# Graph attention on one core: turned tokens between k's units, moments of two graphs per chunk

## The chip, the cores and the metric

The kernel runs on one core of one Trainium2 chip. The metric is the device time of one execution in microseconds; the time before is the median of three runs.

## The reference

128 graphs of 128 tokens with 384 channels. Tokens are normalised and passed through a ReLU, projected to q, k and v, and each graph's 12 heads of 32 channels attend over its 128 tokens, with an adjacency matrix as bias (times beta) and as mask. The result is added to the input.

```python
h = jnp.maximum(_layernorm(x, axis=-1), 0.0)
q = _split_heads(h @ Wq + bq)        # and k, v alike
scores = jnp.einsum('bhqd,bhkd->bhqk', q, k) / jnp.sqrt(HD)
scores = scores + beta * adj_e
scores = jnp.where(adj_e > 0, scores, -9000000000000000.0)
probs = jax.nn.softmax(scores, axis=-1)
out = jnp.einsum('bhqk,bhkd->bhqd', probs, v)
x = x + out.transpose(0, 2, 1, 3).reshape(B, N, D)
```

## The kernel before

**Steps and chunks.** The 128 graphs are taken four at a time in 32 steps (`STEPS`; s is the step, `par` its parity). A step has 12 slots (`SLOTS`), called chunks here and numbered u = 0 to 11. In one chunk the attention of one graph's four heads is worked on (`HPC` = 4; three chunks a graph), while the projections of the step's own four graphs (512 tokens) are worked off between the attention's instructions. The attention of a step's graphs lags: it begins at chunk 3 of the following step (`LAG` = 3). Steps 1 to 30 hold everything: attention of earlier graphs, projections, and preparation of the next step's tokens. Step 0 has no attention, step 31 prepares no tokens, step 32 has only attention.

**The attention's round.** For chunk n: TensorE forms four score tiles in the one PSUM bank `ps_s` (L456), once VectorE has read those of chunk n-1. VectorE adds the mask, negates, and takes each row's minimum (`biased`, `neg_max`, L638, four instructions with an accumulator read each). ScalarE takes the exponentials (`probs`, L523, four). One chunk later TensorE transposes them into `ps_t` (L464), ScalarE rounds them to fp16 (`pT` high, L548), VectorE forms the remainder (`pT` low, L644). One chunk later again TensorE multiplies with v (L479 to L481) into `ps_o`. When a graph's third chunk is through, VectorE takes the reciprocal of the sums (L654) and scales (L659, `on`), GpSimd adds x (L334), and SyncE's queue stores.

**The units of a step.** `UNITS` (L43) lists the other work of TensorE in a step, in order: q0 q1 q2, k0 k1 k2, v0 v1, turn 0, v2, turn 1, v3, turn 2. A q or k unit is nine matmuls of 512 columns, a v unit nine of 384 (high and low parts of both operands: `PARTS`), a turn unit transposes one third of the channels of the next step's normalised tokens `hn` (four transposes, L415). L55 to L71 cut this list into 24 pieces of about equal cost (512 or 384 a matmul, 1024 a turn), two for each chunk; `ENDED[u]` lists the units that end in chunk u. The pieces go out between the attention's instructions (TensorE's `step`, L484 to L497): scores, first piece, transposed probs, second piece, values.

**The banks.** Every unit writes one of three PSUM banks, in rotation over the list and over the step's border (`BANK`, L74). A unit's bank is free when the unit three positions ahead has been read (`bank_free`, L389): for q and k when VectorE has formed the low part (`qk_low`), for v when ScalarE has copied it (`v_copied`), for a turn when VectorE has formed the low part of `hT` (`h_low`).

**Who reads a unit.** ScalarE, in the chunk where the unit ended, behind the exponentials and pT high: high part of q, k (L543), of `hT` (L530), or the copy of v (L538). VectorE, one chunk later, right behind `biased`: `low_parts(s, par, u - 1, ahead)`, that is L619 for q and k, L609 for `hT`. v units ask nothing of VectorE.

**VectorE's order in a chunk** (L663 to L687): `biased`; low parts of the units that ended in the chunk ahead; in chunks 2, 5, 8 and 11 the reciprocal; in chunks 0 to 3 `moments` of one graph of the next step (L586); in chunks 2, 5, 8 and 11 the scaling; in chunk 4 `mask_unlinked` (L598), in chunk 7 `mask_linked` (L603); in chunks 0 to 3 `variance` (L592); pT low.

**GpSimd's order in a step** (L336 to L366): split of the last v (L326, L328), bias added to x of graphs 0 and 1 (L319), the add of graph 2 of two steps ago, bias of graph 2, then `rstd_of` and `normalise` of the next step's tokens (L302 to L313; they wait for all four variances), the add of graph 3, bias of graph 3, the add of graph 0, splits of v0 and v1, the add of graph 1, the split of v2. A turn on TensorE waits for all four normalised graphs (`normed`, L413).

**SyncE's queue** (L257 to L278): two stores, the 12 DMAs that spread q over partitions (they wait for the last low q part), a store, loads of x and adj, a store, the 12 DMAs that spread k.

Of the kernel before, what the change touches and what calls it, by code (L numbers as in the profile page):

```python
# [21 lines left out]
def graph_attention_kernel(nc, x, adj, wq, bq, wk, bk, wv, bv, beta, out):  # L22
# [4 lines left out]
    CH = D // P  # L27
    G = 4
    STEPS = GRAPHS // G
# [10 lines left out]
    assert N == P and TOK == 512 and HPC * N == 512  # L40


    UNITS = ([("q", c) for c in range(CH)] + [("k", c) for c in range(CH)]  # L43
             + [("v", 0), ("v", 1), ("turn", 0), ("v", 2), ("turn", 1), ("v", 3), ("turn", 2)])
    NB = len(UNITS)
    PROJ = [u for u in UNITS if u[0] != "turn"]
    QK = 2 * CH
    NP = len(PROJ)


# [33 lines left out]
    with ExitStack() as ctx:  # L84
# [98 lines left out]
        qk_high = sem("qk_high")  # L183
        qk_low = sem("qk_low")
# [15 lines left out]
        def wait(eng, s, value):  # L200

            if value > 0:
                eng.wait_ge(s, value)
# [83 lines left out]
        @block.gpsimd  # L287
        def _(pool):
            pool.memset(ident[:], 0.0).then_inc(ident_zeroed, 1)
            pool.memset(ones[:], 1.0).then_inc(consts_set, 1)  # L290
            pool.wait_ge(ident_zeroed, 1)
            pool.affine_select(out=ident[:], in_=ident[:], compare_op=ALU.not_equal, fill=1.0, base=0,
                               pattern=[[-1, P]], channel_multiplier=1).then_inc(consts_set, 1)
            pool.memset(half[:], -0.5).then_inc(consts_set, 1)
            pool.wait_ge(consts_set, 3)

            def rstd_of(s):

                wait(pool, var_done, G * (s + 1))
                wait(pool, normed, G * s)  # L300
                pool.nop(nofuse=True)
                pool.tensor_scalar(var_eps[:], mean_var[:, :, 1], EPS, None, ALU.add).then_inc(eps_added, 1)  # L302
                pool.tensor_scalar(neg_mean[:], mean_var[:, :, 0], -1.0, None, ALU.mult).then_inc(eps_added, 1)
                pool.wait_ge(eps_added, 2 * (s + 1))
                pool.tensor_tensor(rstd[:], var_eps[:], half[:], ALU.pow).then_inc(rstd_done, 1)

            def normalise(s, par):

                pool.wait_ge(rstd_done, s + 1)
                wait(pool, h_turned, CH * s)  # L310
                pool.nop(nofuse=True)
                for j in range(G):
                    pool.tensor_scalar(hn[:, j, :], xs[:, par, j, :], neg_mean[:, j:j + 1], rstd[:, j:j + 1],  # L313
                                       ALU.add, ALU.mult).then_inc(normed, 1)

            def add_bias(s, par, j):
                wait(pool, x_in[par], 8 * (s - par) + 16)
                wait(pool, added, G * (s - 2) + j + 1)
                pool.tensor_tensor(xb[:, par, j, :], xs[:, par, j, :], bv_row[:], ALU.add).then_inc(xb_done, 1)  # L319

            def split_v(s, par, j):
                wait(pool, pv_done, SLOTS * (s - 2) + CH * (j + 1))
                pool.wait_ge(v_copied, G * s + j + 1)
                pool.nop(nofuse=True)
                v32 = v_f[:, j % 2].rearrange("p (h d) -> p h d", d=HD)
                pool.tensor_copy(v1[:, par, j, :, 0:HD], v32).then_inc(v_high, 1)  # L326
                pool.wait_ge(v_high, G * s + j + 1)
                pool.tensor_tensor(v2[:, par, j], v32, v1[:, par, j, :, 0:HD], ALU.subtract).then_inc(v_split, 1)  # L328

            def add_x(s, par, j):  # L330

                pool.wait_ge(scaled, G * s + j + 1)
                pool.wait_ge(xb_done, G * s + j + 1)
                pool.tensor_tensor(on[:, j % 2, :], on[:, j % 2, :], xb[:, par, j, :], ALU.add).then_inc(added, 1)  # L334

            def step(s, par):  # L336
                proj, attend = 0 <= s <= STEPS - 1, 1 <= s <= STEPS
                older = 2 <= s <= STEPS
                if 1 <= s <= STEPS:
                    split_v(s - 1, 1 - par, G - 1)  # L340
                if proj:
                    add_bias(s, par, 0)
                    add_bias(s, par, 1)
                if older:
                    add_x(s - 2, par, 2)
                if proj:
                    add_bias(s, par, 2)
                if 0 <= s <= STEPS - 2:
                    rstd_of(s + 1)
                    normalise(s + 1, 1 - par)  # L350
                if older:
                    add_x(s - 2, par, 3)
                if proj:
                    add_bias(s, par, 3)
                if attend:
                    add_x(s - 1, 1 - par, 0)
                if proj:
                    split_v(s, par, 0)
                    split_v(s, par, 1)
                if attend:  # L360
                    add_x(s - 1, 1 - par, 1)
                if proj:
                    split_v(s, par, 2)
                if s == STEPS:
                    add_x(s - 1, 1 - par, 2)
                    add_x(s - 1, 1 - par, 3)  # L366

            rstd_of(0)
            normalise(0, 0)
            w_c = w_raw[:, :, W_COLS[1]]  # L370
            pool.wait_ge(w_squared, 2)
            pool.wait_ge(qk_scaling, 9)
            pool.tensor_tensor(w_c, w_c, gap[:, 1:2, :].bitcast(F32).broadcast_to([P, CH, D]),
                               ALU.mult).then_inc(wk_scaled, 1)
            pool.wait_ge(w_squared, 3)
            pool.wait_ge(v_scaling, 6)
            for c in range(CH):
                w_c = w_raw[:, c, W_COLS[2]].rearrange("p (h d) -> p h d", d=HD)
                pool.tensor_tensor(w_c, w_c, v_scale[:].rearrange("p (h o) -> p h o", o=1).broadcast_to([P, HEADS, HD]),
                                   ALU.mult).then_inc(wv_scaled, 1)  # L380
            for par in range(2):
                for j in range(G):
                    pool.tensor_copy(v1[:, par, j, :, HD], v_scale[:]).then_inc(consts_set, 1)
            pool.wait_ge(bv_in, 16)
            run_steps(step)

        @block.tensor
        def _(pe):
            def bank_free(s, par, o):  # L389

                if s == 0 and o < PB:
                    pe.wait_ge(h_low, o + 1)
                    return
                before, last, here = s, o - 1, par
                while True:
                    if last < 0:
                        before, last, here = before - 1, NB - 1, 1 - here
                    unit = UNITS[last]
                    runs = before < STEPS - 1 or unit[0] != "turn"
                    if runs and BANK[here][last] == BANK[par][o]:  # L400
                        break
                    last -= 1
                kind, n = unit
                if kind == "turn":
                    wait(pe, h_low, CH * (before + 1) + n + 1)
                elif kind == "v":
                    wait(pe, v_copied, G * before + n + 1)
                else:
                    wait(pe, qk_low, QK * before + last + 1)

            def turn(s, bank, c):

# [169 lines left out]
        def _(dve):  # L582
            def moments(s, par, j):
                wait(dve, x_in[par], 8 * (s - par) + 16)
                wait(dve, var_done, G * (s - 1) + j + 1)
                dve.bn_stats(stats[:, j, :], xs[:, par, j, :]).then_inc(stats_done, 1)  # L586
# [26 lines left out]
            def low_part(s, par, o):  # L613

                kind, n = UNITS[o]
                bank = ps_p[BANK[par][o]]
                dve.wait_ge(qk_high, QK * s + o + 1)
                dst, b = (qT, 0) if kind == "q" else (kT, 1)
                dve.scalar_tensor_tensor(out=dst[:, 1, n, :], in0=bank[:], scalar=bias_qk[:, b, n:n + 1],  # L619
                                         in1=dst[:, 0, n, :], op0=ALU.add, op1=ALU.subtract).then_inc(qk_low, 1)  # L620
# [42 lines left out]
            def step(s, par):  # L663
                proj, ahead = 0 <= s <= STEPS - 1, 0 <= s <= STEPS - 2
                for u in range(SLOTS + (LAG + 3 if s == STEPS else 0)):
# [7 lines left out]
                        low_parts(s - 1, 1 - par, SLOTS - 1, s <= STEPS - 1)  # L673
                    if ended:
                        invert_sums(valued[1], valued[3] // CH)
                    if ahead and u < G:
                        moments(s + 1, 1 - par, u)
                    if ended:
                        scale_out(valued[1], valued[3] // CH)
                    if proj and u == 4:  # L680
                        mask_unlinked(s, par)
                    if proj and u == 7:
                        mask_linked(s, par)
                    if ahead and u < G:
                        variance(s + 1, u)
                    if turning:
                        p_low(turning[0], (u - LAG - 1) % 2)  # L687

# [88 lines left out]
```

## Time and profile before

| | |
|---|---|
| median of three runs | 1162.26 us (1161.06 to 1162.73) |
| the profiled execution's own time | 1160.99 us |
| its span | 1159.1 us |
| TensorE matmul, weight load: busy | 1089.7 us (94%), 902.9 us (78%) |
| VectorE busy | 972.2 us (84%) |
| ScalarE busy | 891.0 us (77%) |
| GpSimd busy | 578.6 us (50%) |
| DMA, share of 16 engines | 43.7% (main queue) |
| mean granted TensorE clock | 0.974 |

The profile is of one execution. The span runs from its first to its last instruction; the execution's own time is 1.9 us longer, and 1.27 us below the median of the runs. Matmuls are pipelined and their ends are modelled, so PE's busy share says little about how much of PE is used; the timeline of single instructions says more. A row of the timeline gives start, duration, engine, line, operation, what is written and read, how many instructions are merged, and in brackets the idle time of the engine ahead of it with what ended it.

### The profile page before, as it was taken

What the parts mean: (1) busy time and instruction counts of PE and PEld (TensorE: products, weight loads), DVE (VectorE), ACT (ScalarE), POOL (GpSimd) and SP (SyncE); (2) the same over time, 40 slices, a digit from 0 to 9 for tenths busy, and PEclk for the clock granted to TensorE, in tenths of its full rate; (3) what the DMA queues carried; (4) which work ended last, traced back from release to release, by engine and by line L of the source; (5) the groups of instructions that cost most, each with busy time, mean ns of one, the idle gap of its engine ahead of it and who ended that gap; (6) DMA issues with size and microseconds to landing.
All of it is one profiled execution on the core that took longest, in us unless ns stands there. A gap on an engine that the chain in (4) does not pass through costs nothing. (4 is left out here: it accounts for less than half of the span.)

```text
span 1159.1 us, 33776 instructions
## 1 busy us (share of the span) xinstructions
PE 1089.7 (94%) x10959; PEld 902.9 (78%) x10959; DVE 972.2 (84%) x4343; ACT 891.0 (77%) x2343; POOL 578.6 (50%) x756
## 2 busy tenths in 40 slices
PE   4899999999999999999999999999999999999986
PEld 2778878888878888787888887888888788888764
DVE  6578888888888888898888888888889888888865
ACT  2377888788787888787888878788877888887865
POOL 3735464454555454546545455545454554545331
PEclk9999999999999999999999999999999999999965
DMA  4444434554434455444455443445544444543320
GB/s 145 116 123 123 110 105 123 140 147 126 120 98 123 130 140 136 120 111 113 119 137 147 130 116 100 122 128 139 145 115 109 114 119 134 147 126 98 98 70 28
DMA packets 91038, 138.79 MB, mean 120 GB/s; under 512 B 15600, under 2 KB 66288, under 8 KB 90864
## 3 DMA queue, kind: packets, MB, share of 16 engines
q1 hardware_dynamic: 90336, 135.85, 43.7%
q8 instruction: 88, 1.44, 0.6%
q14 instruction: 86, 0.70, 0.2%
q10 hardware_dynamic: 528, 0.79, 0.2%
HBM read 35.91 MB, written 25.17 MB: 53 GB/s over the span
## 5 line engine op out<-in xcount | busy, mean ns | idle before, releaser
L523 ACT ACTIVATE probs<-biased,neg_max 128x128 f32<-128x128 f32 x1536 | 491.9, 391 | 222.8 <-DVE neg_max L638 186.0
L435 PE MATMUL ps_p<-hT,w 128*128 128x512 f32 x1728 | 527.1, 423 | 5.2 <-DVE qT L619 2.5
L644 DVE TENSOR_TENSOR pT<-ps_t,pT 128x512 f16<-128x512 f32 x384 | 262.9, 685 | 141.3 <-ACT pT L548 141.0
L334 POOL TENSOR_TENSOR on<-on,xb 128x384 f32<-128x384 f32 x128 | 129.2, 1009 | 471.8 <-DVE on L659 392.9
L638 DVE CUSTOM_DVE_ANT_0 biased<-ps_s,mask 128x128 f32<-128x128 f32 x1536 | 352.0, 285 | 6.3 <-PE ps_s L456 4.3
L435 PEld LDWEIGHTS ps_p<-hT,w 128*128 128x128 f32 x1728 | 294.2, 192 | 53.4 <-DVE hT L609 7.3
L435 PE MATMUL ps_p<-w,hT 128*128 128x384 f32 x1152 | 270.2, 357 | 30.4 <-DVE hT L609 30.4
L464 PE MATMUL ps_t<-ident,probs 128*128 128x128 f32 x1536 | 237.8, 279 | 3.1 <-ACT probs L523 1.5
L464 PEld LDWEIGHTS ps_t<-ident,probs 128*128 128x128 f32 x1536 | 193.9, 143 | 43.8 <-ACT probs L523 7.1
L548 ACT ACTIVATE pT<-ps_t 128x512 f16<-128x512 f32 x384 | 220.5, 574 | 1.2 <-PE ps_t L464 1.2
L435 PEld LDWEIGHTS ps_p<-w,hT 128*128 128x128 f32 x1152 | 186.8, 189 | 37.6 <-DVE hT L609 37.5
L479 PEld LDWEIGHTS ps_o<-v,pT 128*128 128x128 f16 x1536 | 122.8, 96 | 84.7 <-issue 73.9
L479 PE MATMUL ps_o<-v,pT 128*128 128x33 f16 x1536 | 160.3, 181 | 3.2 <-DVE pT L644 2.3
L456 PE MATMUL ps_s<-k_st,q_st 96*128 96x128 f16 x1536 | 150.7, 221 | 7.4 <-DVE neg_max L638 4.9
L481 PE MATMUL ps_o<-v,pT 128*128 128x32 f16 x1536 | 155.6, 177 | 0.0
L480 PE MATMUL ps_o<-v,pT 128*128 128x33 f16 x1536 | 155.6, 178 | 0.0
L319 POOL TENSOR_TENSOR xb<-xs,bv_row 128x384 f32<-128x384 f32 x128 | 128.8, 1017 | 8.9 <-POOL on L334 0.4
L638 DVE DVE_READ_ACCUMULATOR2_ANT neg_max<- 128x1 f32 x1536 | 127.7, 83 | 0.1
L480 PEld LDWEIGHTS ps_o<-v,pT 128*128 128x128 f16 x1536 | 125.5, 97 | 0.3
L481 PEld LDWEIGHTS ps_o<-v,pT 128*128 128x128 f16 x1536 | 124.1, 96 | 0.0
L328 POOL TENSOR_TENSOR v<-v_f,v 128x384 f16<-128x384 f32 x128 | 114.0, 891 | 10.3
L456 PEld LDWEIGHTS ps_s<-k_st,q_st 96*128 96x128 f16 x1536 | 90.5, 97 | 10.6 <-DVE neg_max L638 6.2
(62 smaller groups left out, 1034.9 us busy)
## 6 DMA issues: line engine op xcount, KB each, us to landing
q_st<-qT SPq DMA_DIRECT2D x384, 96.0 KB, 2.2
k_st<-kT SPq DMA_DIRECT2D x384, 96.0 KB, 2.2
out<-on SPq DMA_DIRECT2D x128, 192.0 KB, 2.1
xs<-in_x SPq DMA_DIRECT2D x31, 768.0 KB, 4.8
adjs<-in_adj SPq DMA_DIRECT2D x32, 256.0 KB, 5.1
xs<-in_x ACTq DMA_DIRECT2D x1, 768.0 KB, 7.6
k_st<-in_L_gnn_Wq SPq DMA_DIRECT2D x1, 576.0 KB, 5.9
k_st<-in_L_gnn_Wk SPq DMA_DIRECT2D x1, 576.0 KB, 9.2
```

The lines of the kernel that those rows point to most:

```text
L319: pool.tensor_tensor(xb[:, par, j, :], xs[:, par, j, :], bv_row[:], ALU.add).then_inc(xb_done, 1)
L334: pool.tensor_tensor(on[:, j % 2, :], on[:, j % 2, :], xb[:, par, j, :], ALU.add).then_inc(added, 1)
L435: mm = pe.matmul(dst, stationary, moving, start=m == 0, stop=m == MMS - 1)
L456: mm = pe.matmul(ps_s[:, i * N:(i + 1) * N], q_st[0:STACK, gp, i, c, j * N:(j + 1) * N], k_st[0:STACK, gp, i, c, j * N:(j + 1) * N], start ...
L464: mm = pe.transpose(ps_t[odd][:, i * N:(i + 1) * N], probs[:, odd, i, :], ident[:])
L479: pe.matmul(o, high, first, start=True, stop=False)
L480: pe.matmul(o, low, first, start=False, stop=False)
L481: mm = pe.matmul(o[:, 0:HD], high, second, start=False, stop=True)
L523: act.activation(probs[:, odd, i, :], biased[:, odd, i, :], ACT.Exp, bias=neg_max[:, odd, i:i + 1], scale=-1.0).then_inc(exp_done, 1)
L548: act.activation(pT[:, odd, 0], ps_t[odd][:].rearrange("p (h q) -> p h q", q=N), ACT.Copy).then_inc(p_high_done, 1)
L638: dve.tensor_tensor_reduce(out=biased[:, odd, i, :], in0=ps_s[:, i * N:(i + 1) * N], in1=mask[:, gp, v // CH, :], scale=-1.0, scalar=3.0e3 ...
L644: dve.tensor_tensor(pT[:, odd, 1], ps_t[odd][:].rearrange("p (h q) -> p h q", q=N), pT[:, odd, 0], ALU.subtract).then_inc(p_low_done, 1)
```

## The change

Three edits, with what follows from the first. The list of units becomes q0 q1 q2, k0, turn 0, k1, turn 1, k2, turn 2, v0 v1 v2 v3. Since a turn now stands among the k units, the count of q and k units is looked up in a table (`QK_AT`) where the position was used before. VectorE takes moments and variances of two graphs in each of chunks 0 and 1, instead of one in each of chunks 0 to 3. GpSimd runs `rstd_of` and `normalise` ahead of the add of graph 2 and of the bias of graph 2. The 24 pieces are cut anew from the new list by the same rule.

```diff
--- before.py
+++ after.py
@@ -40,11 +40,12 @@
     assert N == P and TOK == 512 and HPC * N == 512
 
 
-    UNITS = ([("q", c) for c in range(CH)] + [("k", c) for c in range(CH)]
-             + [("v", 0), ("v", 1), ("turn", 0), ("v", 2), ("turn", 1), ("v", 3), ("turn", 2)])
+    UNITS = ([("q", c) for c in range(CH)] + [(kind, c) for c in range(CH) for kind in ("k", "turn")]
+             + [("v", j) for j in range(G)])
     NB = len(UNITS)
     PROJ = [u for u in UNITS if u[0] != "turn"]
     QK = 2 * CH
+    QK_AT = {o: [u for u in UNITS if u[0] in "qk"].index(unit) for o, unit in enumerate(UNITS) if unit[0] in "qk"}
     NP = len(PROJ)
 
 
@@ -341,13 +342,13 @@
                 if proj:
                     add_bias(s, par, 0)
                     add_bias(s, par, 1)
+                if 0 <= s <= STEPS - 2:
+                    rstd_of(s + 1)
+                    normalise(s + 1, 1 - par)
                 if older:
                     add_x(s - 2, par, 2)
                 if proj:
                     add_bias(s, par, 2)
-                if 0 <= s <= STEPS - 2:
-                    rstd_of(s + 1)
-                    normalise(s + 1, 1 - par)
                 if older:
                     add_x(s - 2, par, 3)
                 if proj:
@@ -406,7 +407,7 @@
                 elif kind == "v":
                     wait(pe, v_copied, G * before + n + 1)
                 else:
-                    wait(pe, qk_low, QK * before + last + 1)
+                    wait(pe, qk_low, QK * before + QK_AT[last] + 1)
 
             def turn(s, bank, c):
 
@@ -614,7 +615,7 @@
 
                 kind, n = UNITS[o]
                 bank = ps_p[BANK[par][o]]
-                dve.wait_ge(qk_high, QK * s + o + 1)
+                dve.wait_ge(qk_high, QK * s + QK_AT[o] + 1)
                 dst, b = (qT, 0) if kind == "q" else (kT, 1)
                 dve.scalar_tensor_tensor(out=dst[:, 1, n, :], in0=bank[:], scalar=bias_qk[:, b, n:n + 1],
                                          in1=dst[:, 0, n, :], op0=ALU.add, op1=ALU.subtract).then_inc(qk_low, 1)
@@ -673,16 +674,18 @@
                         low_parts(s - 1, 1 - par, SLOTS - 1, s <= STEPS - 1)
                     if ended:
                         invert_sums(valued[1], valued[3] // CH)
-                    if ahead and u < G:
-                        moments(s + 1, 1 - par, u)
+                    if ahead and u < 2:
+                        for j in range(2 * u, 2 * u + 2):
+                            moments(s + 1, 1 - par, j)
                     if ended:
                         scale_out(valued[1], valued[3] // CH)
                     if proj and u == 4:
                         mask_unlinked(s, par)
                     if proj and u == 7:
                         mask_linked(s, par)
-                    if ahead and u < G:
-                        variance(s + 1, u)
+                    if ahead and u < 2:
+                        for j in range(2 * u, 2 * u + 2):
+                            variance(s + 1, j)
                     if turning:
                         p_low(turning[0], (u - LAG - 1) % 2)
```

## Rows read from the trace of the kernel before

**Rows 1.** The page, part 1: busy time, share of the span, instructions of TensorE.

```profile
PE 1089.7 (94%) x10959; PEld 902.9 (78%) x10959; DVE 972.2 (84%) x4343; ACT 891.0 (77%) x2343; POOL 578.6 (50%) x756
```

**Rows 2.** Who waited for whom: total us, times, longest us.

```profile
DVE pT L644 <- ACT pT L548: 141.0, 174, 1.3
...
PE ps_p L435 <- DVE hT L609: 30.4, 30, 1.1
```

**Rows 3.** Timeline of VectorE, chunks 5, 6 and 7 of a middle step: start, us, ...

```profile
544.88 0.28 DVE L638 CUSTOM_DVE_ANT_0 biased<-ps_s,mask 128x128 f32<-128x128 f32 x1
...
547.72 0.28 DVE L638 CUSTOM_DVE_ANT_0 biased<-ps_s,mask 128x128 f32<-128x128 f32 x1
...
549.89 0.69 DVE L644 TENSOR_TENSOR pT<-ps_t,pT 128x512 f16<-128x512 f32 x1 [1.25 <-ACT pT L548]
550.50 0.28 DVE L638 CUSTOM_DVE_ANT_0 biased<-ps_s,mask 128x128 f32<-128x128 f32 x1
...
551.34 0.75 DVE L619 SCALAR_TENSOR_TENSOR kT<-ps_p,bias_qk,kT 128x512 f16<-128x512 f32 x1
552.00 0.74 DVE L603 SCALAR_TENSOR_TENSOR mask<-adjs,beta_col,mask 128x512 f32<-128x512 f32 x1
552.68 0.69 DVE L644 TENSOR_TENSOR pT<-ps_t,pT 128x512 f16<-128x512 f32 x1
553.28 0.28 DVE L638 CUSTOM_DVE_ANT_0 biased<-ps_s,mask 128x128 f32<-128x128 f32 x1
```

**Rows 4.** Timeline of ScalarE, chunk 6 of that step.

```profile
548.10 1.28 ACT L523 ACTIVATE probs<-biased,neg_max 128x128 f32<-128x128 f32 x4 [1.07 <-PE ps_t L464]
549.29 0.57 ACT L548 ACTIVATE pT<-ps_t 128x512 f16<-128x512 f32 x1
```

**Rows 5.** Timeline of TensorE, chunk 10 of that step.

```profile
557.22 0.38 PE L456 MATMUL ps_s<-k_st,q_st 96*128 96x128 f16 x4
...
560.48 0.61 PE L435 MATMUL ps_p<-w,hT 128*128 128x384 f32 x2 [1.09 <-DVE hT L609]
...
561.25 0.38 PE L456 MATMUL ps_s<-k_st,q_st 96*128 96x128 f16 x4
```

**Rows 6.** Timeline of VectorE, chunk 10 of that step and the first of 11.

```profile
558.90 0.28 DVE L638 CUSTOM_DVE_ANT_0 biased<-ps_s,mask 128x128 f32<-128x128 f32 x1
...
559.74 0.69 DVE L609 SCALAR_TENSOR_TENSOR hT<-ps_p,hT 128x512 fp32r<-128x512 f32 x1
...
561.81 0.29 DVE L638 CUSTOM_DVE_ANT_0 biased<-ps_s,mask 128x128 f32<-128x128 f32 x1
```

**Rows 7.** Timeline of VectorE, chunks 0 to 3 of the next step.

```profile
564.61 0.28 DVE L638 CUSTOM_DVE_ANT_0 biased<-ps_s,mask 128x128 f32<-128x128 f32 x1
...
566.05 0.55 DVE L586 BATCH_NORM_STATS2 stats<-xs 128x6 f32<-128x384 f32 x1
566.69 0.18 DVE L592 BATCH_NORM_AGGREGATE mean_var<-stats 128x2 f32<-128x6 f32 x1
...
567.45 0.29 DVE L638 CUSTOM_DVE_ANT_0 biased<-ps_s,mask 128x128 f32<-128x128 f32 x1
...
570.25 0.28 DVE L638 CUSTOM_DVE_ANT_0 biased<-ps_s,mask 128x128 f32<-128x128 f32 x1
...
573.42 0.28 DVE L638 CUSTOM_DVE_ANT_0 biased<-ps_s,mask 128x128 f32<-128x128 f32 x1
...
576.24 0.28 DVE L638 CUSTOM_DVE_ANT_0 biased<-ps_s,mask 128x128 f32<-128x128 f32 x1
```

**Rows 8.** Groups by line, of TensorE: count, busy us, mean ns, idle before.

```profile
L435 PE MATMUL ps_p<-hT,w 128*128 128x512 f32 x1728 | 527.1, 423 | 5.2 <-DVE qT L619 2.5 <-DVE w L725 1.4
...
L435 PE MATMUL ps_p<-w,hT 128*128 128x384 f32 x1152 | 270.2, 357 | 30.4 <-DVE hT L609 30.4
```

**Rows 9.** Timeline of GpSimd in the step of rows 3: normalising.

```profile
543.69 2.81 POOL L313 TENSOR_SCALAR hn<-xs,neg_mean,rstd 128x384 f32<-128x384 f32 x4 [0.21 <-POOL rstd L305]
```

**Rows 10.** Timeline of TensorE, the first scores of all, in step 1.

```profile
59.64 0.38 PE L456 MATMUL ps_s<-k_st,q_st 96*128 96x128 f16 x4 [2.53 <-DMA k_st<-kT]
```

## The prediction

> **What bounds the kernel now.** I read the page first. TensorE (PE) is busy for 94% of the span [rows 1], which invites the reading that PE sets the time and that its gaps are what can be won. The list of waits names the largest gap of PE inside the steps: 30 times, 1.0 us each, it waits for a VectorE instruction that writes hT (the low part of turned tokens), and VectorE in turn waits 174 times, 141 us, for ScalarE's pT before its own pT [rows 2]. So I went to the timeline of one middle step and measured each chunk on VectorE, from one first `biased` to the next. I number chunks by u within the step (12 per step).
>
> Chunk 6 has nothing on VectorE but the attention work. It takes 550.50 - 547.72 = 2.78 us, and VectorE idles 1.25 us of it [rows 3]. What fills it is a round trip: `biased` of this chunk starts; 0.38 us later ScalarE's exponentials start (548.10); after them the high part of the previous chunk's pT (549.29, 0.57 us long) [rows 4]; then VectorE's low pT (549.89), 0.61 us until the next `biased` (550.50) [rows 3]. Every engine queue is in program order, so chunk u+1 can't begin earlier. This loop, at 2.78 us, is the floor of every chunk; PE is ahead of it: the scores of chunk 10 start at 557.22 [rows 5], VectorE takes them up at 558.90 [rows 6], 1.68 us later.
>
> A chunk costs more than 2.78 for one of two reasons. Either VectorE's other work delays its low pT past 2.17 us after the chunk's start: chunk 2 takes 573.42 - 570.25 = 3.17 [rows 7], chunk 5 2.84 [rows 3]. Or PE delivers the next scores late: that is chunk 10, 2.91 us. There PE waits 1.09 us for hT, runs two matmuls of v3, the values and the scores (560.48 to 561.25 [rows 5]), and `biased` starts at 561.81 [rows 6]. So the 1.09 us gap of PE costs the loop only 2.91 - 2.78 = 0.13 us.
>
> **The change, part by part.** I worked out the 24 pieces of a step by the cost rule at lines 55 to 71. Before, turn 0 is in chunk 9, turns 1 and 2 in 10 and 11; after, they lie in chunks 5, 6 and 8, and v0 to v3 end in 9, 10, 11, 11. Each low part is done by VectorE one chunk after its unit ended. No instruction is added or removed, no DMA either; all move.
>
> 1. Moments of two graphs in chunks 0 and 1, none in 2 and 3. Chunk 2 then holds a low q part, the reciprocal and the scaling, just as chunk 5 holds k's: 2.84 in place of 3.17, **-0.33**. Chunk 3 (576.24 - 573.42 = 2.82 [rows 7]) falls to the floor, **-0.04**. Chunk 0 (2.84 [rows 7]) loses the low part of turn 2 (0.60 us of VectorE) and gains one pair of moments. One pair with its variance takes 0.64 us to the variance's start [rows 7]; two take some 0.47 more, since consecutive independent instructions of VectorE start about 0.09 before the recorded end of the one ahead. From 0.84 (end of `biased`) this gives 0.84 + 0.47 + 0.64 + 0.10 = 2.05, below 2.17: covered by the round trip in chunks 0 and 1. Chunk 0 falls to the floor, **-0.06**, chunk 1 from 2.80, **-0.02**. If the cover fails (four instructions end to end: 2 x 0.55 + 2 x 0.18 = 1.46 us instead of 1.21) it is +0.1 for each.
>
> 2. Chunk 10 no longer waits for a turned bank: to the floor, **-0.13**. Chunk 11 (2.80 [rows 6, 7]) loses turn 1's low part: **-0.02**.
>
> 3. The bank wait comes back in chunk 6. Three banks rotate by position, so each unit waits for the one three ahead. Before, v3 (position 11) needed turn 0 (8). After, k2 (position 7) needs turn 0 (4): turn 0 is again in the first half of a chunk, and k2 starts again in the second half of the next, behind turn 1. Turn 0's low part again follows `biased`. So chunk 6 takes on the pattern of chunk 10: 2.91, and k2's two 512-column matmuls instead of v3's 384-column ones: means 423 and 357 ns [rows 8], 2 x 0.066 = 0.13. Chunk 6: 3.04, **+0.26**. Bounds: nothing (k2's start isn't late) and +0.4.
>
> 4. Chunk 7 is the price that I consider decisive. It already has VectorE full: low k part at 551.34, `mask` at 552.00, low pT at 552.68, next `biased` at 553.28 [rows 3], with no idle time. After the change k1 and turn 1 both end in chunk 6, so both low parts stand in chunk 7, ahead of the mask and of low pT. The low part of turned tokens is 0.69 us long [rows 6], of which 0.60 counts (a 0.75 us k part is followed after 0.66 [rows 3]). Nothing covers it: 2.78 + 0.60 = 3.38, **+0.60**. Behind it stand low pT, the next `biased`, and through it ScalarE. Bounds +0.5 and +0.7.
>
> 5. GpSimd. Normalising ends at 543.69 + 2.81 = 546.50 now [rows 9], in chunk 5. It is released two chunks, 5.6 us, sooner, so it ends near 540.9; the first turn after the change, PE's chunk 5, begins no earlier than 544.88 - 1.68 + 0.2 = 543.4 [rows 3, 5, 6]. Slack 2.5 us: nothing. The add of graph 2 that it is moved past (and its store on SP's queue) comes some 3 us later; the buffer is wanted by the scaling of chunk 8 only, and the spread of q behind that store waits for chunk 4 anyway. The two last v parts now end in one chunk, so GpSimd splits them back to back over the step's border: under 6 us into the new step, when the variances come. If all this cover went, PE's turn 0 would wait; the rival below prices it.
>
> 6. Step 0 and 1. Four moments ahead of the first low q part delay PE's first k by about 1 us, and turn 0 then waits for normalising. But PE waits 2.53 us at the first scores for the k_st DMA [rows 10], which begins no later: nothing, bounds -1 and +1.5 us.
>
> **Sum** per full step: -0.33 - 0.04 - 0.06 - 0.02 - 0.13 - 0.02 + 0.26 + 0.60 = +0.26 us. The 30 steps that both attend and look ahead give 7.8 us. Against the profiled execution's own 1160.99 that is 1168.8; its time stands 1.27 below the median of the runs, so by the median 1162.26 the forecast is **1170.1 us**, 0.7% slower.
>
> **A rule that speaks for the change.** Here the busiest engine's gap costs 0.13 of its 1.09 us [rows 5, 6]. The Trainium skill (Perfetto Trace Analysis, Identifying the Most-Contended Engine, with Optimization Strategy) says to take the engine of the highest occupancy and remove what its gaps wait for; it also warns that matmul busy time is a poor measure. By that rule PE's 30 us would be the prize; the trace disagrees.
>
> **Rivals.**
> - *PE sets the pace* (5%): the hT wait [rows 2] vanishes and its 30.4 us with it: 1132. For: 94% busy. Against: the 1.68 us by which PE leads the loop, and the wait's return in chunk 6.
> - *The overloaded chunk is made up for* (10%): VectorE and ScalarE are both late after chunk 7, have idle time in chunks 9 to 11, and regain the 0.60. The sum is then -0.34 a step: 1152, **faster**. It decides where the chunks behind an overloaded one fall below 2.78. Against: behind chunk 2 with its 3.17, chunk 3 still takes 2.82 [rows 7].
> - *No return of the bank wait in chunk 6* (10%): turn 0's low part is in time, the sum is 0.00: 1162, no change. It needs PE to lead by less than 0.6 us there; against it is the lead of 1.68 before chunk 10.
> - *Turned tokens late* (10%): GpSimd isn't done by chunk 5, or chunks 0 and 1 overflow. One chunk's length of 0.2 to 0.4 more per step: 1176 to 1182.
>
> **The numbers.** Forecast 65%, slower by over 0.2%, as is the last rival: 0.75. Within 0.2% (about what a measurement of this kernel can tell from no change): 0.10. Faster: 0.15. The range takes the forecast with its bounds (chunk 6 at +0.4, a tenth in chunks 0 and 1: 0.26 + 0.14 + 0.2, 1180; I stop at 1177, as both at once are unlikely) and, below, the case of no change: 1162 to 1177.
>
> **What would show it.** Right: chunk 7 near 3.4 and chunk 2 near 2.84 on VectorE; PE still waits for hT about 30 times, 0.6 to 1.2 us each, now before k2; chunk 10 at the floor; normalising ends before chunk 5. Wrong: a hT wait gone from PE's list, a chunk 7 under 3.1, chunks behind it under 2.7, or GpSimd's hn named as PE's releaser.

## Result and profile after

The changed kernel takes 1169.68 us (median of 4 runs, 1169.38 to 1170.34), the kernel before 1161.8 us beside it: ratio on record 1.0072, 95% interval 1.0061 to 1.0084 (the two medians alone divide to 1.0068). It is slower by 0.7%, as forecast (1170.1, 0.7%). The spans of the two profiles differ by 1167.5 - 1159.1 = 8.4 us.

From the page, part 1 (busy time and share of the span):

```profile
PE 1089.2 (93%) x10959; PEld 899.8 (77%) x10959; DVE 980.3 (84%) x4343; ACT 893.3 (77%) x2343; POOL 572.5 (49%) x756
```

TensorE does the same work [rows 1]; no engine's busy time tells where 8 us came from. VectorE's is 8.1 us higher with the same instructions, but that is a coincidence: the rise is spread thinly over all its groups, while the time went into two chunks, as the table below shows. From the list of waits (total us, times, longest us), the rows that answer to [rows 2]:

```profile
DVE pT L645 <- ACT pT L549: 143.7, 204, 1.6
...
PE ps_p L436 <- DVE hT L610: 24.1, 30, 1.2
PE ps_p L436 <- ACT v_f L539: 16.5, 15, 1.2
```

The wait for turned tokens has not gone: 30 times again, 24.1 us for 30.4. In the trace it is 1.17 us in odd steps and 0.47 us in even ones. A third row is new in this size: 15 times, 1.1 us each, TensorE waits for ScalarE's copy of v.

VectorE's timeline, chunks 6, 7 and the first of 8 of a middle step (answering to [rows 3, 6]):

```profile
550.03 0.28 DVE L639 CUSTOM_DVE_ANT_0 biased<-ps_s,mask 128x128 f32<-128x128 f32 x1
...
550.87 0.69 DVE L610 SCALAR_TENSOR_TENSOR hT<-ps_p,hT 128x512 fp32r<-128x512 f32 x1
552.21 0.69 DVE L645 TENSOR_TENSOR pT<-ps_t,pT 128x512 f16<-128x512 f32 x1 [0.66 <-ACT pT L549]
553.06 0.29 DVE L639 CUSTOM_DVE_ANT_0 biased<-ps_s,mask 128x128 f32<-128x128 f32 x1 [0.16 <-PE ps_s L457]
...
553.91 0.75 DVE L620 SCALAR_TENSOR_TENSOR kT<-ps_p,bias_qk,kT 128x512 f16<-128x512 f32 x1
554.58 0.68 DVE L610 SCALAR_TENSOR_TENSOR hT<-ps_p,hT 128x512 fp32r<-128x512 f32 x1
555.17 0.74 DVE L604 SCALAR_TENSOR_TENSOR mask<-adjs,beta_col,mask 128x512 f32<-128x512 f32 x1
555.83 0.69 DVE L645 TENSOR_TENSOR pT<-ps_t,pT 128x512 f16<-128x512 f32 x1
556.43 0.28 DVE L639 CUSTOM_DVE_ANT_0 biased<-ps_s,mask 128x128 f32<-128x128 f32 x1
```

Chunk 6 lasts 553.06 - 550.03 = 3.03 us, and its end is a wait for scores. Chunk 7 lasts 556.43 - 553.06 = 3.37 us: two low parts, the mask and low pT follow each other without idle time. Both were 2.78 before. In the even steps, where TensorE waits only 0.47 us in chunk 6, that chunk takes 3.03 us too: already here the length of the wait is not its cost.

The same chunk 6 on TensorE (answering to [rows 5]):

```profile
549.84 0.60 PE L416 MATMUL ps_p<-ident,hn 128*128 128x128 f32 x4
551.61 0.73 PE L436 MATMUL ps_p<-hT,w 128*128 128x512 f32 x2 [1.17 <-DVE hT L610]
...
552.50 0.38 PE L457 MATMUL ps_s<-k_st,q_st 96*128 96x128 f16 x4
```

Turn 1 goes out, k2 waits 1.17 us for turn 0's low part (550.87 + 0.69 = 551.56), and the scores follow 0.89 us after k2's start.

VectorE's timeline at the start of the next step, chunks 0 to 3 (answering to [rows 7]):

```profile
567.64 0.28 DVE L639 CUSTOM_DVE_ANT_0 biased<-ps_s,mask 128x128 f32<-128x128 f32 x1
...
568.48 1.02 DVE L587 BATCH_NORM_STATS2 stats<-xs 128x6 f32<-128x384 f32 x2
569.41 0.36 DVE L593 BATCH_NORM_AGGREGATE mean_var<-stats 128x2 f32<-128x6 f32 x2
...
570.48 0.29 DVE L639 CUSTOM_DVE_ANT_0 biased<-ps_s,mask 128x128 f32<-128x128 f32 x1
...
573.28 0.28 DVE L639 CUSTOM_DVE_ANT_0 biased<-ps_s,mask 128x128 f32<-128x128 f32 x1
...
576.11 0.28 DVE L639 CUSTOM_DVE_ANT_0 biased<-ps_s,mask 128x128 f32<-128x128 f32 x1
...
578.91 0.28 DVE L639 CUSTOM_DVE_ANT_0 biased<-ps_s,mask 128x128 f32<-128x128 f32 x1
```

Chunks 0 to 3 last 2.84, 2.80, 2.83 and 2.80 us. Two pairs of moments end by 569.77, ahead of low pT: covered. Chunk 2 is down from 3.17.

Worked out from both timelines for all of steps 3 to 30 (mean time from one first `biased` to the next, in us):

| chunk | 0 | 1 | 2 | 3 | 4 | 5 | 6 | 7 | 8 | 9 | 10 | 11 |
|---|---|---|---|---|---|---|---|---|---|---|---|---|
| before | 2.84 | 2.80 | 3.18 | 2.83 | 2.80 | 2.83 | 2.79 | 2.79 | 2.84 | 2.79 | 2.92 | 2.80 |
| after | 2.82 | 2.80 | 2.83 | 2.81 | 2.80 | 2.83 | 3.05 | 3.38 | 2.84 | 2.79 | 2.80 | 2.79 |

A step goes from 34.19 to 34.54 us in the mean, 0.35 more. Steps 2 to 30 together take 1001.7 us for 991.6, 10.1 more. The first scores of all come 1.8 us sooner (57.87 for 59.64 [rows 10]); step 1 gains another 0.4 and the two last steps lose 0.4. Together that is the 8.4 us of the spans.

Not all of the 0.35 is the change's. In step 32, which has only attention, a chunk lasts 2.789 us in this trace and 2.781 to 2.783 in the other eleven, among them the five of this same kernel with a small edit. Seven thousandths in each of 12 chunks are 0.08 us a step; why this execution has them stays open. That leaves about 0.27 for the change.

The same step 32 shows what the floor of a chunk is not. TensorE is granted half its clock there (0.50 from 1125 to 1150 us) and has no projections, and every chunk still takes the 2.78 or 2.79 us of a quiet chunk of the full steps. So neither TensorE nor the amount of other work sets the floor; that it is the round trip of `biased`, exponentials, high pT and low pT is read from the timelines, and no run shortens that trip.

### The profile page after: what moved, and what is told of

It is laid out like the page before. It is cut to its first block and busy times, and to the rows that moved or that the text cites. A ratio compares the mean times of both kernels' runs of the same rounds, so it can differ in the third digit from the quotient of the medians.

```text
span 1167.5 us, 33776 instructions
## 1 busy us (share of the span) xinstructions
PE 1089.2 (93%) x10959; PEld 899.8 (77%) x10959; DVE 980.3 (84%) x4343; ACT 893.3 (77%) x2343; POOL 572.5 (49%) x756
## 5 line engine op out<-in xcount | busy, mean ns | idle before, releaser
L436 PE MATMUL ps_p<-hT,w 128*128 128x512 f32 x1728 | 530.0, 423 | 45.8 <-DVE hT L610 24.1
L436 PEld LDWEIGHTS ps_p<-hT,w 128*128 128x128 f32 x1728 | 291.1, 191 | 91.3 <-DVE hT L610 31.2
L436 PE MATMUL ps_p<-w,hT 128*128 128x384 f32 x1152 | 261.9, 354 | 0.0
L327 POOL CAST v<-v_f 128x384 f16<-128x384 f32 x128 | 64.9, 507 | 112.3 <-issue 102.5
```

The lines of the kernel that those rows point to most:

```text
L436: mm = pe.matmul(dst, stationary, moving, start=m == 0, stop=m == MMS - 1)
```

## The experiments

Each was timed against the kernel before on its own chip; I give that ratio and the interval. Means of chunks are taken over steps 3 to 30, as above. The theory under test: every chunk is a round trip VectorE, ScalarE, VectorE of at least 2.79 us, and what a chunk takes beyond it, by VectorE's work or by late scores, is never regained.

**a1_mask6**: the changed kernel, chunk 7 relieved.

```diff
-                    if proj and u == 7:
+                    if proj and u == 6:
                         mask_linked(s, par)
```

> The changed kernel with one edit: the second half of the mask (mask_linked) is taken in chunk 6 instead of chunk 7. The loop theory (every chunk lasts at least 2.79 us, a VectorE overload in one chunk adds to the time in full and is never regained): chunk 7 holds biased 0.84, two low parts 0.66 and 0.60, low pT 0.60, so it falls from 3.37 to 2.79; in chunk 6 the mask (0.68) fits behind turn 0's low part while PE's scores are awaited, so chunk 6 stays 3.03. 30 x 0.58 = 17 us off: 1152, faster than both kernels. Rival, the cost lies in TensorE's waits and not in VectorE's chunk 7: within 2 us of 1169.7. Rival, a late chunk is made up for behind it: the same, within 2 us of 1169.7.

Measured: 1151.35 us, ratio 0.993 (0.9916 to 0.9945): faster than the kernel before, against 1.0072 with the mask in chunk 7. Chunk 7 on VectorE, from its first `biased` to the next:

```profile
545.20 0.29 DVE L639 CUSTOM_DVE_ANT_0 biased<-ps_s,mask 128x128 f32<-128x128 f32 x1 [0.16 <-PE ps_s L457]
...
547.99 0.28 DVE L639 CUSTOM_DVE_ANT_0 biased<-ps_s,mask 128x128 f32<-128x128 f32 x1
```

2.79 us, as computed; chunk 6 stays 3.03. The two ratios differ by 1.4%, some 16.5 us, for the 17 expected. Both rivals fall: the instruction moved by one chunk, no work went, and the late chunk had not been made up for.

**a2_one_each**: the changed kernel, moments one graph a chunk again, and the variances alike.

```diff
-                    if ahead and u < 2:
-                        for j in range(2 * u, 2 * u + 2):
-                            moments(s + 1, 1 - par, j)
+                    if ahead and u < G:
+                        moments(s + 1, 1 - par, u)
...
```

> The changed kernel with the moments put back to one graph in each of chunks 0 to 3 (units and GpSimd's order as changed). The loop theory: chunk 2 goes from 2.83 back to 3.17, chunk 3 by 0.03, and now the tokens are late: the last variance ends some 2.2 us into chunk 3, normalising takes GpSimd some 5 us more, so turn 0 in PE's chunk 5 waits over 2 us and chunk 5 grows by about 1.7; some 2 us a step, 1225 to 1235. Rival, GpSimd is in time anyway and only chunk 2 pays: 0.37 x 30 = 11 us, 1181. Rival, where the moments stand makes no difference: 1170.

Measured: 1275.55 us, ratio 1.1001 (1.0979 to 1.1023). The direction is right, the size is not: 40 us above the top of the range. On TensorE, turn 0 of one step and turn 1 of the same:

```profile
601.86 1.08 PE L416 MATMUL ps_p<-ident,hn 128*128 128x128 f32 x4 [3.15 <-POOL hn L314]
605.59 0.38 PE L457 MATMUL ps_s<-k_st,q_st 96*128 96x128 f16 x4
607.23 0.60 PE L416 MATMUL ps_p<-ident,hn 128*128 128x128 f32 x4
```

The stretch from 600 to 604 us (busy times, then the granted clock):

```profile
600.00:604.00 4.00, 2.14 (x8) 1.87 (x9) 2.40 (x12) 1.33 (x5) 3.86 (x6) 0.66 0.10 37
```

After waiting 3.15 us TensorE was granted 0.66 of its clock there, so a part of the stretch ran at the 1.2 GHz level: four transposes take 1.08 us instead of 0.60, and the next scores start 3.73 us after the turn does, for 2.56 in the changed kernel. Chunk 5 lasted 6.2 us in odd and 5.6 us in even steps on average, not the 4.5 that I had worked out at full clock. The steps themselves separate the wait from the clock. In steps 6, 12, 14, 16, 18 and 24 TensorE waited 2.6 to 2.9 us and its clock stayed at 1.00 throughout chunk 5: the chunk took 4.7 us. In the other 23 of steps 2 to 30 it waited 2.6 to 3.2 us, the clock fell, and the chunk took 5.8 to 6.9 us. All six are even steps, and beside the even steps with the same wait the lower clock costs 1.3 to 2.2 us. So with the clock at full my sum was near, 4.7 for 4.5, and the lower clock is most of the missing 40 us; in odd steps, where the wait was 3.0 to 3.2 us, the clock fell every time, so the two aren't told apart there. The Trainium skill (TensorE: Matmul & The Clock Gate, What's actually happening) says that the clock follows how busy the array has lately been; this row agrees: TensorE had been idle for 3.15 us. The 1.17 us wait of the changed kernel doesn't do this: its clock in that stretch is 1.00.

So the units' new order needs tokens so early that the moments must come first: with GpSimd's order but without the moments edit it costs 10%. Whether it needs GpSimd's order too, no run tries. An estimate from the rows of the changed kernel says yes: with the add and the bias of graph 2 ahead of it, normalising could begin no sooner than 575.60 (end of VectorE's scaling) + 1.01 + 1.02 = 577.63, where it began at 572.81; it would end near 582.1 instead of 577.3, and turn 0 starts at 581.04, so it would be some 1.1 us late.

**b1_moments_only**: the kernel before with the moments edit of the diff alone.

> The kernel before with the moments edit alone (two graphs in each of chunks 0 and 1; old units, old order of GpSimd). The loop theory: chunk 2 from 3.17 to 2.84 and chunk 3 by 0.03 shorter, but chunk 0 still holds the low part of turn 2: 0.84 + 0.60 + 0.47 + 0.64 + 0.10 + 0.60 = 3.25, 0.41 over 2.84. Sum +0.04 a step, no change: 1161 to 1164. Rival, the moments edit is a gain by itself and the order of units the whole cost: 0.37 x 30 = 11 us off, 1151.

Measured: 1158.27 us, ratio 0.9992 (0.9983 to 1.0002), no change. Chunk 0 on VectorE:

```profile
562.31 0.28 DVE L638 CUSTOM_DVE_ANT_0 biased<-ps_s,mask 128x128 f32<-128x128 f32 x1
...
563.15 0.69 DVE L609 SCALAR_TENSOR_TENSOR hT<-ps_p,hT 128x512 fp32r<-128x512 f32 x1
563.75 1.01 DVE L586 BATCH_NORM_STATS2 stats<-xs 128x6 f32<-128x384 f32 x2
564.68 0.36 DVE L592 BATCH_NORM_AGGREGATE mean_var<-stats 128x2 f32<-128x6 f32 x2
564.95 0.66 DVE L644 TENSOR_TENSOR pT<-ps_t,pT 128x512 f16<-128x512 f32 x1
565.53 0.28 DVE L638 CUSTOM_DVE_ANT_0 biased<-ps_s,mask 128x128 f32<-128x128 f32 x1
```

3.22 us for the 3.25 computed. What chunk 2 gains (0.35) chunk 0 pays (0.37), both in the mean. It is the old turn 2, whose low part falls into chunk 0, that makes the same edit worthless here and a gain in the changed kernel.

**b2_chunk2_free**: the kernel before, moments and variances put where the round trip covers them.

```diff
-                    if ahead and u < G:
-                        moments(s + 1, 1 - par, u)
+                    for j in (((0,), (1, 2), (), (3,))[u] if ahead and u < 4 else ()):
+                        moments(s + 1, 1 - par, j)
...
```

> The kernel before with moments of graph 0 in chunk 0, graphs 1 and 2 in chunk 1, graph 3 in chunk 3, none in chunk 2. The loop theory: chunk 1 has room for two (low pT may start at 2.17, they end by 2.05), so chunk 1 stays 2.80, chunk 2 falls from 3.17 to 2.84, the rest stays: 0.33 x 30 = 10 us off, 1152. Rival, VectorE's chunk lengths are not what sets the step (its work is only moved, and it is idle elsewhere): 1162.

Measured: 1149.05 us, ratio 0.9911 (0.9896 to 0.9925), 10.1 us less than the kernel before on that chip, as computed. Chunks 1 and 2:

```profile
560.74 0.29 DVE L638 CUSTOM_DVE_ANT_0 biased<-ps_s,mask 128x128 f32<-128x128 f32 x1
...
563.53 0.28 DVE L638 CUSTOM_DVE_ANT_0 biased<-ps_s,mask 128x128 f32<-128x128 f32 x1
...
566.37 0.28 DVE L638 CUSTOM_DVE_ANT_0 biased<-ps_s,mask 128x128 f32<-128x128 f32 x1
```

2.79 and 2.84 us. Two instructions a step, the moments and the variance of graph 2, moved by one chunk; no unit touched.

**b3_mask6**: the kernel before with the mask's edit of a1_mask6.

> The kernel before with mask_linked in chunk 6 instead of chunk 7. The loop theory: chunk 7 was full but exactly at the floor (2.78), and chunk 6 has 1.25 us idle, so 0.68 us less in one and more in the other changes nothing: ratio 0.999 to 1.001. Rival, every busy microsecond of VectorE in a full chunk counts: 0.6 x 30 = 18 us off, ratio 0.985.

Measured: 1159.67 us, ratio 1.0001 (0.9992 to 1.001). The same edit gives 16 us to the changed kernel and nothing to this one, since chunk 7 was full but not over the floor.

**a3_cut**: the changed kernel, one matmul of k2 fewer in chunk 6.

```diff
-            ATOMS.append((o, 0, 2 * TOK))
+            ATOMS.append((o, 0, 3 * TOK))
```

> The changed kernel with one number changed: a turn counts 3 x 512 instead of 2 x 512 when the units are cut into pieces. By this only one matmul of k2 instead of two goes out in chunk 6, and no unit ends in another chunk. The loop theory: in chunk 6 the chain biased, low part of turn 0, k2's matmuls, values, scores, biased loses one matmul of 512 columns, 0.24 us: 3.03 to 2.80. 30 x 0.24 = 7 us off the changed kernel: 1163, a ratio of 1.001 to the kernel before. Rival, PE's wait itself (1.1 us in odd, 0.5 in even steps) is the cost of chunk 6: it is as long as before, so no change: ratio 1.007.

Measured: 1162.88 us, ratio 1.0031 (1.0019 to 1.0042), between the two expectations and nearer to the loop's. Chunk 6 on TensorE and on VectorE:

```profile
548.58 0.50 PE L436 MATMUL ps_p<-hT,w 128*128 128x512 f32 x1 [1.29 <-DVE hT L610]
549.24 0.38 PE L457 MATMUL ps_s<-k_st,q_st 96*128 96x128 f16 x4
```

```profile
547.00 0.28 DVE L639 CUSTOM_DVE_ANT_0 biased<-ps_s,mask 128x128 f32<-128x128 f32 x1
...
549.79 0.29 DVE L639 CUSTOM_DVE_ANT_0 biased<-ps_s,mask 128x128 f32<-128x128 f32 x1
```

TensorE waits longer, 1.29 us in odd steps for 1.17, and yet the chunk falls to 2.79 here and to 2.82 in the mean. The length of the wait isn't the cost; what stands between its end and the next scores is. Most of the missing 0.002: chunk 1 of every even step rose from 2.81 to 2.90, since the new cut gives it eight 512-column matmuls where TensorE has just lost its lead.

**a4_cut_mask6**: both edits.

> The changed kernel with the same cut (a turn counts 3 x 512) and mask_linked in chunk 6. The loop theory: both gains add, since they are in different chunks: 0.58 + 0.24 = 0.82 us a step off the changed kernel, 25 us: 1145, ratio 0.986. In chunk 6 the mask follows turn 0's low part and is not in the chain. Rival, with so much less in the loop PE becomes the bound (its lead was shrinking): ratio 0.990 or more.

Measured: 1149.16 us, ratio 0.991 (0.9893 to 0.9926): only 0.002 better than a1_mask6, intervals overlapping. The loop theory's 0.986 is missed and the rival's 0.990 or more came. TensorE in chunk 7:

```profile
542.46 0.38 PE L457 MATMUL ps_s<-k_st,q_st 96*128 96x128 f16 x4
542.65 1.18 PE L436 MATMUL ps_p<-hT,w 128*128 128x512 f32 x4
543.67 0.60 PE L465 MATMUL ps_t<-ident,probs 128*128 128x128 f32 x4
544.02 1.18 PE L436 MATMUL ps_p<-hT,w 128*128 128x512 f32 x4
545.36 0.38 PE L457 MATMUL ps_s<-k_st,q_st 96*128 96x128 f16 x4
```

Eight matmuls make it 2.90 us long. With a lead this is hidden (chunk 2 of the changed kernel has eight too, and lasts 2.83), but right behind a wait there is none, and chunk 7 lasts 2.90 on VectorE as well. Of the 0.21 us that chunk 6 gained over a1_mask6, chunks 7 (0.09) and 1 (0.05 in the mean) gave most back: the cut moved a matmul to where TensorE was the bound. So the loop theory holds only where TensorE has a lead; without one, a chunk of eight 512-column matmuls has a floor of its own, 2.90.

**a5_cut4_mask6**: mask in chunk 6 and a turn counted `4 * TOK`.

> The changed kernel with mask_linked in chunk 6 and a turn counted 4 x 512. Turn 0 then ends in chunk 4 beside k0, so its low part is in time for k2 and PE's wait in chunk 6 is gone; but chunk 5 holds two low parts, reciprocal and scaling: 0.84 + 0.66 + 0.60 + 0.25 + 0.48 + 0.60 = 3.43 in place of 2.83. The loop theory: +0.60 and -0.24 a step against the kernel with mask_linked in chunk 6 alone (ratio 0.993): 11 us more, ratio 1.002, though PE waits less. Rival, PE's waits for turned tokens are the cost: ratio 0.987 (7 us less).

Measured: 1164.82 us, ratio 1.0045 (1.003 to 1.006). From a1_mask6's 0.993 that is 13 us more, 11 expected. Chunk 5 on VectorE:

```profile
545.55 0.28 DVE L639 CUSTOM_DVE_ANT_0 biased<-ps_s,mask 128x128 f32<-128x128 f32 x1
...
548.98 0.28 DVE L639 CUSTOM_DVE_ANT_0 biased<-ps_s,mask 128x128 f32<-128x128 f32 x1
```

3.43 us as computed, and chunk 6 is 2.79 in odd and 2.81 in even steps. The 2 us over the forecast have a cause that I had not reckoned with: chunk 0 of every even step rose from 2.85 to 3.07, 15 x 0.22 = 3.4 us. There TensorE waits 1.05 us for the copy of v before q0 (the wait of point 6 below), and the new cut puts eight matmuls of q0 behind it instead of seven. An overload costs in full in another chunk too, and turned tokens that come in time don't repay it.

**b4_old_units**: the changed kernel with the old list of units.

> The changed kernel with the old list of units: moments edit and GpSimd's new order stay. The loop theory: as the moments edit alone, chunk 0 at 3.21 and chunk 2 at 2.83, and GpSimd's order costs nothing: ratio 0.998 to 1.001. So the new list of units would carry the whole slowdown. Rival, normalising ahead of the adds delays stores and the spread of q, and GpSimd's order has a part in the slowdown: ratio 1.002 or more.

Measured: 1158.15 us, ratio 0.9986 (0.9976 to 0.9995). GpSimd's new order costs nothing that shows beside b1_moments_only (0.9992). The list of units carries the whole slowdown, 1.0072 against 0.9986.

**c1_best**: b2_chunk2_free with another end of the list.

```diff
-             + [("v", 0), ("v", 1), ("turn", 0), ("v", 2), ("turn", 1), ("v", 3), ("turn", 2)])
+             + [("v", 0), ("turn", 0), ("v", 1), ("v", 2), ("turn", 1), ("v", 3), ("turn", 2)])
```

> The kernel before with moments in chunks 0 (one), 1 (two) and 3 (one), and the units v0, turn 0, v1, v2, turn 1, v3, turn 2 at the end of the list. Turn 0 then ends in chunk 8, its low part stands in chunk 9, and turn 1 and v3 in chunk 10 find their banks free; no chunk holds more work of VectorE than before (chunk 10 loses a low part, chunk 9 gets one and stays at the floor). The loop theory: chunk 10 from 2.91 to 2.79, on top of the 0.33 of chunk 2; as PE's lead isn't lost in chunk 10, every second step may pay 0.05 at q0's bank. 0.33 + 0.12 - 0.03 a step: 12 to 13 us, ratio 0.988 to 0.990. Rival, PE is now the bound and its wait was only idle time that it had anyway: ratio as with the moments alone, 0.991, or worse.

Measured: 1155.49 us, ratio 0.9964 (0.9952 to 0.9977): not the best but worse than b2_chunk2_free. Chunk 8 on TensorE:

```profile
550.59 0.80 PE L435 MATMUL ps_p<-w,hT 128*128 128x384 f32 x3 [0.77 <-DVE kT L619]
551.54 0.38 PE L456 MATMUL ps_s<-k_st,q_st 96*128 96x128 f16 x4
```

Chunk 10 did fall to 2.79, but v1 now stands three behind k2, whose low part is due in this very chunk, and three matmuls of v1 follow the wait: chunk 8 rose from 2.84 to 3.15. I had checked the banks of turns and v3 and not v1's, the same mistake of kind that the change makes with k2.

## Why the prediction was right

1. **Moments.** Forecast -0.33 for chunk 2, -0.04, -0.06 and -0.02 for chunks 3, 0 and 1; measured -0.35, -0.02, -0.02 and 0.00. The cover in chunks 0 and 1 held; for chunk 1 b2_chunk2_free shows it alone. The term of chunk 0 was wrong in its cause. The one chunk 0 that I had read (2.84) is of an even step; in the kernel before, the median is 2.84 in even steps and 2.79 in odd ones, and after the change it is the same. The 0.05 was never the low part of turn 2 but TensorE's, by the wait of point 6, and it stayed; the -0.02 of the means comes from a few single long chunks of the kernel before.

2. **Chunk 10** -0.13, measured -0.11; chunk 11 -0.02, measured -0.01.

3. **The bank wait returns in chunk 6**: forecast 3.04, measured 3.03 in the step shown, 3.05 in the mean. That not the wait's length but the matmuls behind it count is shown by a3_cut, and by the even steps with their wait of 0.47 us, which is below the 0.6 that I had named as a sign.

4. **Chunk 7**: forecast 3.38, measured 3.37 in the step shown, 3.38 in the mean. a1_mask6 shows it by removal, a5_cut4_mask6 by the same overload in another place.

5. **GpSimd**: forecast to cost nothing; b4_old_units agrees. Normalising ended at 577.31 and turn 0 began at 581.04, a slack of 3.7 us for the 2.5 forecast. That tokens two chunks later are too late is shown by a2_one_each.

6. **What I missed inside the step.** TensorE waits 1.1 us for v's copy at the start of every even step. I took the three banks to rotate on over the step's border, and the section on the kernel before says so too; they don't. `BANK` knows only the step's parity, 13 units a step make 26 for two, and 26 is not a multiple of 3: from an odd step to an even one q0 stands on the bank of position 11. That was v3 and is now v2, both copied in chunk 11. Before, chunk 10's wait had taken TensorE's lead, so it arrived late and hardly waited; now the scores of chunk 0 start 1.7 us ahead of their `biased` (565.96 and 567.64), before 0.7. ScalarE's and TensorE's rows:

```profile
566.91 0.85 ACT L539 ACTIVATE v_f<-ps_p 128x384 f32<-128x384 f32 x2
```

```profile
565.96 0.38 PE L457 MATMUL ps_s<-k_st,q_st 96*128 96x128 f16 x4
567.43 1.20 PE L436 MATMUL ps_p<-hT,w 128*128 128x512 f32 x4 [1.09 <-ACT v_f L539]
```

The cost to the loop is small, 2.84 for 2.79 in every second step, and it isn't new: before, q0 started 0.05 us behind the end of v3's copy (564.39 behind 564.34), now 0.05 behind the end of v2's (567.43 behind 567.38), and the first `biased` of chunk 1 comes 3.06 and 3.05 us after q0's start. So 16.5 us of new waiting on TensorE cost nothing; what they show is a lead that it didn't have.

7. **Start**: forecast nothing, bounds -1 and +1.5; measured -1.8, outside. First k did come later (36.73 for 36.02) and turn 0 did wait for normalising. But I had the k_st spread begin no later, and it began sooner. SyncE's queue after:

```profile
38.09 7.57 SPq L249 DMA_DIRECT2D q_st<-qT  x12
...
48.24 7.50 SPq L249 DMA_DIRECT2D k_st<-kT  x12
```

k_st starts at 48.24, it was 49.20, and the first scores no longer wait. That is 1 us of the gain; why the q_st spread took 7.57 us to issue instead of 9.07, and where the other 0.8 us came from, stays open.

That the total came within half a microsecond is partly luck: 0.35 a step against 0.26 forecast would be 2.7 us more, most of it in an execution that was slower in every chunk, and the start gave 1.8 us back by a path that was forecast as nothing. The two large terms, chunk 6 and chunk 7, and the large gain, chunk 2, were right in mechanism and in size.

Of the rivals, "PE sets the pace" and "made up for" fell with a1_mask6, a3_cut and a5_cut4_mask6; "no return of the bank wait" with the trace; "turned tokens late" did not occur here, but a2_one_each shows it to be real, and far dearer than I had priced it: 3.1 us a step in chunk 5, not 0.2 to 0.4.

Fastest are b2_chunk2_free and a4_cut_mask6, 0.9% below the kernel before and not told apart; the first needs only the moments moved.

## What to carry to other kernels

Where engines hand work round in a fixed order, find the round trip's length first and cost every chunk against it: work below that line is free, work above it counts in full and is not regained. Then count TensorE's matmuls in each chunk: behind a wait it has no lead, and one matmul more there lengthens the chunk. When units that share buffers are reordered, list for each unit who must have released its buffer and in which slot that happens, over the loop's border too; and of a wait that returns, price only what stands between its end and the next hand-over. The engine that waits looks guilty in the list of waits, and its wait may cost a tenth of its length.

## What the runs showed of the hardware that I had not expected

In a2_one_each waits of TensorE of 2.6 to 3.2 us brought the granted clock down to its 1.2 GHz level in 23 of steps 2 to 30 and left it at 1.00 in six; the six waited 2.6 to 2.9 us, and so did nine of the 23, so within this range the length of the wait doesn't say which it will be. Between steps with the same wait, the fall made the chunk 1.3 to 2.2 us longer. In the kernel before, the one wait of 2.53 us [rows 10] was followed by a fall as well (0.50 at 62 us). The waits of up to 1.2 us of the changed kernel, some 30 of them, left its clock at 1.00 from 41 to 1122 us.

In b3_mask6 the mask instruction took twice its time. VectorE and GpSimd in chunk 6:

```profile
547.96 1.43 DVE L603 SCALAR_TENSOR_TENSOR mask<-adjs,beta_col,mask 128x512 f32<-128x512 f32 x1
```

```profile
547.84 1.01 POOL L319 TENSOR_TENSOR xb<-xs,bv_row 128x384 f32<-128x384 f32 x1
```

Its median over the 32 steps is 1.43 us, in chunk 7 of the kernel before 0.74 [rows 3]. Here GpSimd had started an add 0.12 us earlier. The traces hold the same pair at other distances:

| GpSimd's add starts | mask takes, us | add takes, us | where |
|---|---|---|---|
| no add beside it | 0.74 | | before, 31 steps; after, all 32 |
| 0.73 us ahead of the mask | 0.82 | 1.00 | a1_mask6, most steps |
| 0.45 us ahead | 1.10 | 1.00 | a1_mask6, one step |
| 0.12 us ahead | 1.43 | 1.00 | b3_mask6, most steps |
| 0.17 us behind | 0.75 | 1.45 | b3_mask6, one step |

When the add starts first, the mask ends 0.55 us after the add does, whatever the distance; when the mask starts first, it keeps its 0.75 us and the add pays. The Trainium skill (SBUF — State Buffer, SBUF: two separate sides) calls the port pair of VectorE and GpSimd an exclusive lock, which a VectorE instruction with two SBUF inputs also has to take; these rows agree with it, but for some 0.2 us: after the add the mask needs 0.55 us more, not its whole 0.74. The loss cost nothing in b3_mask6 only because chunk 6 had 1.25 us to spare: low pT still started 2.19 us into the chunk. The mask had filled this room with 1.35 us instead of 0.68.
